# An adapter projection and a per-head MLP on one core: groups of two against quads with merged blocks, and three edits at the start and the end

## The reference

```python
w = weight[adapter_ids]                       # 16 x 1024 x 1024, 8 picked
y = einsum('bsi,boi->bso', x, w)
t = y[..., perm].reshape(tokens, 16, 64)
t = gelu(einsum('bhd,hdm->bhm', t, up))       # up 16 x 64 x 256
t = einsum('bhm,hmd->bhd', t, down)           # down 16 x 256 x 64
out = x + t.reshape(tokens, 1024)[..., argsort(perm)]
```

## Time and profile before

| | us |
|---|---|
| device time, median of 3 runs | 301.78 (300.81 to 303.13) |
| the profiled execution's own device time | 302.47 |
| its span from first to last instruction | 300.6 |
| TensorE matmul busy | 293.7 |
| VectorE busy | 177.6 |
| ScalarE busy | 159.0 |
| GpSimd busy | 98.7 |

### The profile page before, as it was taken

How to read it: one execution, slowest core, us unless ns; L and a number is a source line. 1 busy time by engine, 2 the same in 40 slices (tenths; PEclk the granted TensorE clock), 3 DMA queues, 4 the chain that set the end, 5 groups by cost and what they waited for, 6 DMA issues and landing times.

```text
span 300.6 us, 4303 instructions
## 1 busy us (share of the span) xinstructions
PE 293.7 (98%) x1672; PEld 211.3 (70%) x1672; DVE 177.6 (59%) x210; ACT 159.0 (53%) x179; POOL 98.7 (33%) x92
## 2 busy tenths in 40 slices
PE   8999999999999999999999999999999999999994
PEld 3778888888888758586685857858587685544441
DVE  2778769769765963594736847466564723333332
ACT  3637336347439462854429363392824507777750
POOL 3000000188250064181632617130471535222234
PEclk9999999999999999999999999999999999999998
DMA  6999999999996878579675767755376193421335
GB/s 201 324 426 422 420 419 409 317 338 394 393 365 231 340 269 324 177 247 324 221 293 209 277 237 267 271 195 190 120 253 222 70 303 120 136 73 70 139 142 209
DMA packets 23555, 77.87 MB, mean 259 GB/s; under 512 B 2672, under 2 KB 11248, under 8 KB 18544
## 3 DMA queue, kind: packets, MB, share of 16 engines
q1 hardware_dynamic: 6912, 43.39, 39.2%
q0 software_dynamic: 7488, 25.18, 23.4%
q10 hardware_dynamic: 9136, 9.05, 8.8%
HBM read 60.82 MB, written 16.78 MB: 258 GB/s over the span
## 4 chain that ended last, share of the span: by engine, by line
PE 91%; DMA 3%; SPq 2%; issue 1%; DVE 1%; POOL 1%; ACT 0%; POOLq 0%; DVEq 0%
PE ps L535 38%; PE ps L536 19%; PE ps L584 18%; PE ps L563 6%; PE ps L566 5%; PE ps L569 5%; DMA w_raw<-w 3%; SPq L217 1%; POOL out_late L286 1%; SPq L194 1%; DVE w_lo L405 0%; ACT w_hi L317 0%; DVE w_raw L438 0%; SPq L223 0%; POOLq L307 0%
## 5 line engine op out<-in xcount | busy, mean ns | idle before, releaser
L535 PE MATMUL ps<-x_pair,w_hi 128*128 128x512 f32 x480 | 171.0, 401 | 0.7 <-DVE w_lo L405 0.7
L536 PE MATMUL ps<-x_pair,w_lo 128*128 128x256 f32 x480 | 134.7, 281 | 0.0
L535 PEld LDWEIGHTS ps<-x_pair,w_hi 128*128 128x128 f32 x480 | 90.2, 188 | 29.9 <-issue 7.2
L351 ACT ACTIVATE hidden<-ps 128x1024 f32<-128x1024 f32 x64 | 61.0, 1030 | 63.3 <-PE ps L569 56.6
L317 ACT ACTIVATE w_hi<-w_raw 128x1024 fp32r<-128x1024 f32 x60 | 60.4, 1060 | 60.4 <-PE ps L536 32.3
L536 PEld LDWEIGHTS ps<-x_pair,w_lo 128*128 128x128 f32 x480 | 90.6, 189 | 0.0
L405 DVE TENSOR_TENSOR w_lo<-w_raw,w_hi 128x1024 fp32r<-128x1024 f32 x60 | 70.7, 1219 | 13.6 <-ACT w_hi L317 13.6
L259 POOL DMA_INDIRECT t_raw<-y_rows,idx x32 | 33.6, 1049 | 107.7 <-DMA y_rows<-y_out 86.1
L429 DVE TENSOR_REDUCE y_out<-ps 128x256 f32<-128x512 f32 x64 | 42.6, 686 | 41.1 <-PE ps L536 28.5
L584 PE MATMUL ps<-hidden,down_sb 128*64 128x512 f32 x256 | 58.2, 598 | 0.0
L584 PEld LDWEIGHTS ps<-hidden,down_sb 128*64 128x64 f32 x256 | 17.0, 136 | 33.4 <-issue 33.0
(11 more groups left out here) (28 smaller groups left out, 112.5 us busy)
## 6 DMA issues: line engine op xcount, KB each, us to landing
w_raw<-w SPq DMA_DIRECT2D x30, 1024.0 KB
y_rows<-y_out ACTq DMA_DIRECT2D x32, 256.0 KB
x_raw<-x_cols SPq DMA_DIRECT2D x7, 1024.0 KB, 8.0
w_raw<-w SPq DMA_DIRECT2D x4, 256.0 KB, 4.8
hidden<-up SPq DMA_DIRECT2D x1, 1024.0 KB, 10.0
down_sb<-down SPq DMA_DIRECT2D x1, 1024.0 KB, 9.8
w_raw<-w SPq DMA_DIRECT2D x2, 384.0 KB, 7.1
x_raw<-x_cols ACTq DMA_DIRECT2D x2, 256.0 KB, 3.6
```

Source lines behind the costliest of these rows:

```text
L351: nc.scalar.activation(hidden[:, f % HS, m, :, :], up_banks(f, m)[:, :, :], ACT.Gelu).then_inc(gelu_done, 1)
L535: nc.tensor.matmul(acc, w_hi[:, ws, k, col], x_pair[:, xs, k, :, :], start=(k == 0), stop=False)
L536: last = nc.tensor.matmul(acc[:, 0, :], w_lo[:, ws, k, col], x_hi[:, xs, k, :], start=False, stop=(k == KT - 1))
```

## The change

1. **Quads and blocks.** The lists are over quads q of four projection units. Behind quad q = 2 comes the up of head pair 0 alone. Behind quads 3 to 6 (block k = q - 2) comes up pair 2k-1, down pair 2k-2, down pair 2k-1, up pair 2k. Quad 7 has no block behind it, and then up pair 9, down pair 8, and so on as before. PSUM banks and the waits for them are assigned anew: a unit of quads 1 and 2 waits for the sum of the unit one or two before it in the first half of a quad; the first pair's up waits for the sums of all twelve units; a unit of a quad behind a block waits for the gelu that reads its banks. `x_high`, `x_low` stand ahead of unit 4q+2's sum up to quad 2, and at the head of the quad behind that. `w_high`/`w_low(g+2)` follow unit g (its sum, on VectorE) for the first three units of a quad, and `w_high`/`w_low(4q+5)` the block. GpSimd's list is rewritten to the same order. `down_unit` waits for each gelu ahead of the products that read it.
2. **Unit 2's weights by halves.** The first half's high and low conversion is moved ahead of the quads; on VectorE it now precedes `y_sum(0)`, the second half follows it. The first half on ScalarE waits for unit 0's third piece (`first_half_done`) in place of unit 0's end.
3. **x's third piece later.** ScalarE's queue issues it after the first `x_high`.
4. **Last head unit halved.** f = 31's down runs over columns 0 to 255 and then 256 to 511, into two banks, with one add for each.

The diff, cut to its core (the lists are those of ScalarE, then VectorE, then, behind the waits of `lora_unit` and `up_unit`, TensorE):

```diff
-PAIR, LEAD = 2, 6
+PAIR, QUAD, LEAD = 2, 4, 2
+QUADS = NL // QUAD
+BLOCKS = QUADS - LEAD - 1
+TURNS = 2 * BLOCKS - 1
+UP_QUAD, UP_UNITS = 2, (0, 2)
...
+        def y_bank(g, o):
+            return ps[2 * ((g // QUAD + g % QUAD // 2) % 2) + g % 2][:, o, :].rearrange("p (c s) -> p c s", c=2)
...
+            for n in range(X_AHEAD):
+                load_first_x(n)
...
                 first_x_high(n)
+                if n == 0:
+                    for later in range(X_AHEAD, X_BY_ACT):
+                        load_first_x(later)
...
+            w_high_half(PAIR, 0)
+            for q in range(QUADS):
+                k = block_behind(q)
+                for g in lora_of(q):
+                    if q >= LEAD and g % QUAD == (0 if q > LEAD else QUAD - 1):
+                        for f in units(2 * (q - LEAD) - 1 if q > LEAD else 0):
+                            t_high(f)
+                    if g % QUAD == (0 if q > LEAD else 2) and q + 1 < B:
+                        x_high(q + 1)
+                    if g % QUAD < 3 and g + 2 < NL:
+                        w_high(g + 2)
+                    y_park(g)
+                    if q == UP_QUAD and g % QUAD in UP_UNITS:
+                        up_high(UP_UNITS.index(g % QUAD))
+                if k:
+                    for f in units(2 * k - 1):
+                        gelu(f)
+                        t_high(f + PAIR)
+                if QUAD * q + 5 < NL:
+                    w_high(QUAD * q + 5)
+                if k is not None:
+                    for f in units(2 * k):
+                        gelu(f)
...
+            w_low_half(PAIR, 0)
+            for q in range(QUADS):
+                k = block_behind(q)
+                for g in lora_of(q):
+                    if q >= LEAD and g % QUAD == (0 if q > LEAD else QUAD - 1):
+                        for f in units(2 * (q - LEAD) - 1 if q > LEAD else 0):
+                            t_low(f)
+                    if g % QUAD == (0 if q > LEAD else 2) and q + 1 < B:
+                        x_low(q + 1)
+                    y_sum(g)
+                    if g % QUAD < 3 and g + 2 < NL:
+                        w_low(g + 2)
+                    if q == UP_QUAD and g % QUAD in UP_UNITS:
+                        up_low(UP_UNITS.index(g % QUAD))
...
+                if q > LEAD:
+                    f = PAIR * 2 * (q - LEAD - 1) + g % QUAD // 2
+                    pe.wait_ge(gelu_done, MT * f + g % 2 + 1)
+                elif q > 0:
+                    pe.wait_ge(y_summed, OT * (g - 1 if g % QUAD < 2 else g - 5))
...
+                if behind_quad:
+                    pe.wait_ge(y_summed, OT * (QUAD * q + (4 if p == 0 else 2 * (f % 2 + 1))))
...
+            for q in range(QUADS):
+                k = block_behind(q)
+                for g in lora_of(q):
+                    if g >= PAIR:
+                        lora_unit(g)
+                if k:
+                    for f in units(2 * k - 1):
+                        up_unit(f)
+                    for f in units(2 * k - 2):
+                        down_unit(f)
+                    for f in units(2 * k - 1):
+                        down_unit(f)
+                if k is not None:
+                    for f in units(2 * k):
+                        up_unit(f)
```

More of the change, by code:

```diff
@@ L39 @@
 X_AHEAD = 2
+HALF_PIECE = 2
+LAST_PAIR = 1
 WARM = 4
@@ L393, in _, with w_low_half @@
+            for p in range(TURNS, PAIRS):
+                for f in units(p):
                     gelu(f)
-                    if split_ahead(j):
+                    if p + 1 < PAIRS:
                         t_high(f + PAIR)
-                if j + 1 < L_GROUPS:
-                    w_high(PAIR * (j + 1) + 1)
         @block.vector
         def _(dve):
+            def w_low_half(g, n):
+                k = slice(n * HALF, (n + 1) * HALF)
+                dve.wait_ge(w_hi_done, 2 * (g - PAIR) + n + 1)
+                nc.vector.tensor_tensor(w_lo[:, g % WS, k, :], w_raw[:, g % WRAW, k, :],
+                                        w_hi[:, g % WS, k, :].bitcast(F32), ALU.subtract).then_inc(w_lo_done, 1)
@@ L436, in add_x @@
                     dve.wait_ge(rows_in[f % XR], 16 * (f // XR + 1))
-                dve.wait_ge(down_done, f + 1)
-                nc.vector.tensor_tensor(row_place(f), down_bank(f), row_place(f), ALU.add).then_inc(added, 1)
+                for n, tok in enumerate(token_parts(f)):
+                    dve.wait_ge(down_done, f + n + 1)
+                    last = nc.vector.tensor_tensor(row_place(f)[:, tok], down_place(f, n), row_place(f)[:, tok], ALU.add)
+                last.then_inc(added, 1)
             def first_x_low(n):
@@ L461, in _ @@
             first_w_low(1, PIECES - 1)
-            for j in range(GROUPS):
-                if j > 0:
-                    for f in down_of(j - 1):
-                        add_x(f)
-                if j < L_GROUPS:
-                    if j > 0:
-                        w_low(PAIR * j + 1)
-                    if PAIR * j % LPB == PAIR and PAIR * j // LPB + 1 < B:
-                        x_low(PAIR * j // LPB + 1)
-                    for f in up_of(j):
-                        t_low(f)
-                    y_sum(PAIR * j)
-                    if up_of(j):
-                        y_sum(PAIR * j + 1)
-                    if j + 1 < L_GROUPS:
-                        w_low(PAIR * (j + 1))
-                    if j in UP_GROUPS:
-                        up_low(UP_GROUPS.index(j))
-                    if not up_of(j):
-                        y_sum(PAIR * j + 1)
-                if split_ahead(j):
-                    for f in up_of(j):
-                        t_low(f + PAIR)
-            for f in down_of(GROUPS - 1):
+            w_low_half(PAIR, 0)
[13 more added lines that the diff above has]
+                if k:
+                    for i in range(PAIR):
+                        t_low(PAIR * 2 * k + i)
+                        add_x(PAIR * (2 * k - 2) + i)
+                    for f in units(2 * k - 1):
+                        add_x(f)
+                if QUAD * q + 5 < NL:
+                    w_low(QUAD * q + 5)
+            for p in range(TURNS, PAIRS):
+                if p + 1 < PAIRS:
+                    for f in units(p + 1):
+                        t_low(f)
+                for f in units(p - 1):
+                    add_x(f)
+            for f in units(PAIRS - 1):
                 add_x(f)
@@ L494, in warm @@
                 for n in range(WARM):
-                    nc.tensor.matmul(ps[0][:, 1, :], ones[:, 0:P], ones, start=True, stop=True)
+                    nc.tensor.matmul(ps[3][:, 1, :], ones[:, 0:P], ones, start=True, stop=True)
             def first_lora_piece(g, n):
@@ L511, in first_lora_piece @@
                         last.then_inc(lora_done, 1)
+                if g == 0 and n == HALF_PIECE:
+                    last.then_inc(first_half_done, 1)
             def lora_unit(g):
```

164 lines of the change are left out of this document (93 added, 71 removed).

## The result

| | before | after |
|---|---|---|
| device time, median (lowest to highest), 22 runs each | 302.02 (300.57 to 303.46) | 303.56 (301.98 to 305.30) |
| ratio after / before, 95% interval | | 1.0054 [1.0038, 1.0069] |
| span of the profiled execution | 300.6 | 302.3 |
| its mean granted TensorE clock | 0.997 | 0.992 |

The change costs 0.54% by the ratio, 1.6 us (1.5 between the medians). The forecast was +1.65 us, 303.4, with a span of 302.2. The number is right, and most of its terms are in the trace, but two things took part that stood only among the rivals. In the profiled execution they nearly cancelled: a drop of the clock (about +1.1 net) and a quicker pace of the projection units (−0.9).

A forecast was written before the change was run, and what follows sets the result against it. TensorE, busy 293.7 of 300.6 us, was taken to bound the kernel. Terms -1.4 + 0 + 2.1 + 0.4 + 0.8 - 0.2 + 0.15 - 0.2 = +1.65 us gave 303.4 us from the median 301.78; range 302.0 to 304.8.

The forecast's parts named there:

- Joints: Switches between projection, up and down matmuls on TensorE: fewer per block, gaining 0.36 us in each of four, -1.4 us.
- Blocks free of stalls: Blocks behind quads 3 to 6: all waits covered, tightest by 0.6 us, so 0; a rival with stalls gave +4 us.
- First up: First block: the first up waits for unit 11's sum, last in VectorE's queue, +2.1 us (+1.3 to +2.5).
- Unit 12 and the gelu: After the first up pair: unit 12 waits for the first gelu to free its banks, +0.4 us (0 to +0.8).
- Halves: Inside unit 2: y_sum(0) between the two low halves makes the second late, so TensorE stalls, +0.8 us.
- −0.2** at unit 4: At 31.09 us: unit 2's delay gives w_low(4) time, so the old 0.21 us wait goes, -0.2 us.
- x's third piece: Early transfers: moving the 256 KB piece later leaves a hole that shifts unit 2's weights' landing, +0.15 us.
- Tail: End of the kernel: with the last head unit halved the last add takes 0.42 instead of 0.69 us, -0.2 us.
- The clock: Rival: the first block's stall sends TensorE to 1.2 GHz for some 4 us of work, +2 us, 305.4; chance 0.1.
- slow passes of ones: Before the first matmuls: eight warm-up passes took 5.6 us where 1.7 is full pace, cited beside the clock drop.
- Pace: Rival: projection units keep 0.347 us a matmul pair instead of 0.353, -3.1 us over 30 units; chance 0.09.
- It never came back after other joints: The prediction's argument against projection units keeping the faster matmul pace of units 2 and 3.

The follow-up runs named there:

- rep_after: The changed kernel run once more without an edit, for its profile: 302.20 us, span 300.4.
- e_nohalf: The changed kernel with part 2 undone, unit 2's halves converted in a row behind y_sum(0): 303.64 us, ratio to before 1.0064.
- e_xearly: The changed kernel with part 3 undone, x's third piece issued with the others: 303.11 us, ratio to before 1.0059.
- e_whole_last: The changed kernel with part 4 undone, the last head unit whole, a single run: 303.25 us, span 301.5.
- e_upq1: The changed kernel with the up weights' conversions one quad earlier, behind units 4 and 6: 301.88 us, ratio to before 0.9998.
- e_banks: e_upq1 plus quad 2's units taking their PSUM bank pairs in the other order: 302.03 us, ratio to before 1.0001.
- rep_wait: e_wait run once more without a further edit: 303.39 us, span 301.6.
- e_wait: The changed kernel with a spare VectorE reduction behind up_low(1) that the first up waits for: 304.05 us, ratio to before 1.0067.
- e_gelu: e_banks plus ScalarE doing head unit 0's gelu ahead of unit 13's high weights: 300.89 us, ratio to before 0.9977.

## Why the prediction was right, and where it was not

- **Joints** (−1.4): right. 0.35 a block, four times; 0.36 was predicted.
- **Blocks free of stalls** (0): right. No wait in any block of after, and 35.77 in all four.
- **First up** (+2.1): right, 2.1 to 2.3 in five profiles. Place, releaser and queue were as predicted. The chain from `x_low`'s start came out at 8.08, as summed, and `x_low` started 4.1 us after unit 9's end, as reckoned. The 0.2 on top is pace: at 0.346 us a pair unit 11 was through 11.1 us after unit 9, not 11.3. The profiles that run at 0.353 up to there have a wait of 2.1 (`rep_after`, `e_nohalf`), those at 0.346 have 2.3 (after, `e_xearly`, `e_whole_last`). `e_upq1` shows the cause of the wait: one task less in front of the sum, 1.1 us less wait.
- **Unit 12 and the gelu** (+0.4): right as a size in every profile with that wait in which the clock held, and incomplete as a picture. I had priced what shows behind the first wait. The chain sum, park, high weights, gelu is itself late by 1.4 us against a first up without a wait (`e_banks`). Whoever costs a repair from the prediction's list would take 2.1 for the first wait and get about 1.1.
- **Halves** (+0.8): 0.77 in the profile, 0.26 to 0.83 over those of after and its near variants. The mechanism, a sum between two low halves, was right; the size hangs on how early TensorE gets to unit 2, counted from the landing of its weights. I took 19.68, the time of before, when it had waited for the weights. In after it came at 19.56 without a wait, because its own first units ended then: real matmuls began at 7.58, before at 6.88. What of it reaches the end is not settled, as undoing it gave no measurable time. The **−0.2** at unit 4 came.
- **x's third piece** (+0.15): not seen. The Trainium skill's sentence (DMA: Bandwidth & Descriptors, Issuing engines are not separate DMA queues), by which moving it saves issue time alone, fits better than my term: ScalarE's start on unit 2's weights stays within 16.06 to 17.49 us either way.
- **Tail** (−0.2): −0.27 in the profile, −0.31 against `e_whole_last`.
- **The clock**: the step that failed is its chance of 0.1. It fell in 14 of 22 runs of after, so it is the likelier case, and it belonged in the sum. I priced it at +2, with some 4 us of work at half pace. It lasted 3.4 us and cost 1.55, of which 0.4 would have been waited anyway. The argument that no row excluded it was right and should have given it far more weight. The slow passes of ones that stood beside it are no support: the profile shows a granted clock of 1.00 there (1.00 from 0 to 8 us in after as well), and why they take 5.6 us is open. The Trainium skill (TensorE: Matmul & The Clock Gate, HAM oscillation) warns of idle gaps between bursts; these runs agree in kind, with gaps of 2.1 to 2.3 us.
- **Pace**: given 0.09 as a fixed gain for the kernel. It is no property of the kernel: both values occur in both kernels. "It never came back after other joints" holds for that profile alone: in `rep_after` the faster pace begins at unit 12, and in `rep_wait` it comes back at unit 16. In after's profile it gave −0.9.

Put together again with what is now known: −1.4 + 2.2 + 0.4 + 0.26 to 0.8 − 0.2 − 0.3 gives about +1.0 to +1.5 where the clock holds, and 1.05 more where it falls. The median spans are about 300.2 (before: its 302.02 less the 1.8 that lie around the program), 301.0 and 302.05, that is +0.8 and +1.9. Weighted by 8 and 14 of 22 they give +1.5, as the medians do. So the forecast met the time in part by luck: a drop in most runs made up for terms that were some tenths of a us too high; how the latter split up is below what these medians resolve.

## What to carry to other kernels

Where a merged or reordered stage waits for the unit right before it, count the list in front of that unit's last task on each engine, and follow the same event through every queue that depends on it: here two engines hung on one sum, and repairing VectorE's side alone gave 1.1 us where the list of waits promised 2.1. Putting matmuls of one kind together saved about 0.18 us for each joint less, small but certain, while one wait of 2 us undid it and in over half of the runs took the clock along. And a sum that meets the time is not yet a sum whose terms are right: compare stretch by stretch, in more than one execution.

## What the runs showed of the hardware

- TensorE's granted clock fell to 1.2 GHz for about 3.4 us at idle stretches of 2.1 to 2.3 us in 23 of 44 runs and of 3.4 us in 5 of 6 (by the mean clock of the run; four profiles show the place), and in none of 106 runs whose longest was 1.4 us or less. It fell 0.8 to 1.5 us after work resumed in two profiles with 2.1 to 2.3 us and 0.6 us after it in one with 3.4 us, but 0.5 us before the idle stretch ended in the other (`e_wait`). I had expected it to be rare at 2 us.
- The matmul pairs of a projection unit (512 and 256 columns) run at 0.346 or 0.353 us in stretches that change from one execution to the next of the same kernel, at full granted clock; 0.11 us a unit, up to 3.4 us over 30 units. In all 14 profiles the pace stays as it is while the projection runs on, for up to 56 us, and changes only where TensorE's work was broken by a wait or by another kind of matmul: at the wait of 0.21 us at 31.09 in before, at the one of 0.49 us before unit 14 in `e_gelu` (0.353 ahead of it, 0.346 behind), at the first up in after. Many breaks leave it as it is. Within the blocks behind quads 3 to 6 an up pair took 2.94 to 3.0 and two down pairs 7.01 to 7.02 at either. What sets it is open; no run was made on it.
- From the first pass of ones (1.46 in every profile) to the first real matmul it took 4.7 to 6.1 us in the profiles of these kernels, with the passes unchanged (1.46 to 7.58 in after, to 6.62 in `rep_after`).
